# Running a step's three Q or K products in one go, with residual adds drawn apart and splits of x behind them, in a graph attention kernel

## The reference, cut to what matters

```python
def reference(x, adj, Wq, bq, Wk, bk, Wv, bv, Wf, bf):     # x (128,128,384), adj (128,128,128) bool
    q, k, v = heads(x @ Wq + bq), heads(x @ Wk + bk), heads(x @ Wv + bv)      # 6 heads of 64
    scores = einsum('bhqd,bhkd->bhqk', q, k) / sqrt(64)
    probs  = softmax(scores + where(adj, 0, -9e15)[:, None])
    ctx    = einsum('bhqk,bhkd->bhqd', probs, v)            # heads joined again to 384
    return layernorm(x + ctx @ Wf + bf)                     # over the 384, eps 1e-5, no affine
```

## Time and profile before

| | |
|---|---|
| median of 3 runs | 1035.22 us (1034.44 to 1036.75) |
| the profiled execution, its own time | 1036.09 us |
| its span, first to last instruction | 1034.2 us |
| TensorE busy | 98% of the span, 7161 matmuls |
| VectorE, ScalarE, GpSimd busy | 71%, 57%, 61% |
| mean granted TensorE clock | 0.997 of full |
| DMA | 179.6 MB, 174 GB/s in the mean |

### The profile page before, as it was taken

One profiled execution on the slowest core, in us unless ns is written; L12 is line 12 of the kernel. 1 busy time (PEld: TensorE's weight loads), 2 busy tenths in 40 slices (PEclk: granted clock), 3 DMA queues, 4 the chain that ended last, 5 costly groups with the idle time before them and its releaser, 6 DMA issues.

```text
span 1034.2 us, 26752 instructions
## 1 busy us (share of the span) xinstructions
PE 1018.6 (98%) x7161; PEld 906.7 (88%) x7161; DVE 734.0 (71%) x2826; ACT 592.9 (57%) x2119; POOL 626.8 (61%) x649
## 2 busy tenths in 40 slices
PE   8999999999999999999999999999999999999995
PEld 7889889888889888888898898898898898888885
DVE  3677776777677677777777777767776777776775
ACT  4565655655656646646556556556556466466551
POOL 1355666666656665665656656666566566656674
PEclk9999999999999999999999999999999999999998
DMA  7386676676676676666666766766766766765444
GB/s 196 79 210 178 173 197 163 176 189 163 177 190 163 180 189 166 186 181 167 189 174 172 194 167 173 196 162 175 191 161 174 195 164 182 185 167 171 152 141 139
DMA packets 340570, 179.63 MB, mean 174 GB/s; under 512 B 222656, under 2 KB 324160, under 8 KB 340544
## 3 DMA queue, kind: packets, MB, share of 16 engines
q1 hardware_dynamic: 339744, 178.94, 63.4%
q10 hardware_dynamic: 800, 0.39, 0.1%
HBM read 103.75 MB, written 75.50 MB: 173 GB/s over the span
## 4 chain that ended last, share of the span: by engine, by line
PE 96%; DVE 1%; DMA 1%; ACT 0%; issue 0%; POOL 0%; SPq 0%; POOLq 0%; DVEq 0%; ACTq 0%
PE qk_ps L377 14%; PE qk_ps L379 13%; PE qk_ps L378 13%; PE cov_ps L377 13%; PE cov_ps L379 13%; PE cov_ps L378 13%; PE scores_ps L393 9%; PE cov_ps L408 9%; DMA p_out<-p_turned 1%; DVE s_mask L572 1%; PE qk_ps L468 0%; POOL probs L870 0%; SPq L289 0%; DVE xT_lo L561 0%; ACT probs L755 0%
## 5 line engine op out<-in xcount | busy, mean ns | idle before, releaser
L755 ACT ACTIVATE probs<-s_mask,neg_max 128x128 f32<-128x128 f32 x768 | 297.5, 391 | 6.2 <-DVE neg_max L578 5.5
L870 POOL TENSOR_TENSOR probs<-probs,inv_sum 128x768 f32<-128x768 f32 x128 | 188.9, 1476 | 81.5 <-DVE inv_sum L591 81.5
L572 DVE CUSTOM_DVE_ANT_0 s_mask<-scores_ps,mask_bias 128x128 f32<-128x128 f32 x768 | 172.5, 286 | 91.5 <-PE scores_ps L393 86.5
L865 POOL TENSOR_SCALAR y_sb<-y_sb,mean_var,rstd 128x384 f32<-128x384 f32 x124 | 204.9, 1652 | 22.9 <-POOL rstd L859 22.9
L584 DVE STREAM_TRANSPOSE p_turned<-probs 128x768 f32<-128x768 f32 x128 | 125.2, 978 | 114.2 <-POOL probs L870 114.0
L859 POOL TENSOR_TENSOR rstd<-var_eps,minus_half 128x1 f32<-128x1 f32 x128 | 72.0, 563 | 181.8 <-DVE var_eps L619 181.8
L772 ACT ACTIVATE qT<-qk_ps,bq_col 128x512 f32<-128x512 f32 x96 | 65.5, 682 | 155.5 <-PE qk_ps L379 155.5
L755 ACT ACTIVATION_READ_ACCUMULATOR probs<-s_mask,neg_max 128x1 f32 x768 | 145.0, 189 | 0.0
L748 ACT CAST cT_hi<-cov_ps 128x384 fp32r<-128x384 f32 x128 | 61.5, 480 | 137.2 <-PE cov_ps L408 134.3
L561 DVE TENSOR_TENSOR xT_lo<-xT,xT_hi 128x384 fp32r<-128x384 f32 x120 | 113.1, 980 | 32.8 <-ACT xT_hi L742 32.7
L377 PE MATMUL cov_ps<-wf_hi,cT_hi 128*128 128x384 f32 x384 | 129.9, 338 | 1.7 <-DVE cT_lo L546 1.7
(11 more groups left out here) (64 smaller groups left out, 1988.5 us busy)
## 6 DMA issues: line engine op xcount, KB each, us to landing
p_out<-p_turned SPq DMA_DIRECT2D x128, 384.0 KB, 2.6
pT<-p_out SPq DMA_DIRECT2D x512, 96.0 KB, 2.4
x_in<-in_x SPq DMA_DIRECT2D x128, 192.0 KB, 3.6
out<-y_sb SPq DMA_DIRECT2D x128, 192.0 KB, 2.5
x_blocks<-in_x SPq DMA_DIRECT2D x360, 64.0 KB, 2.3
adj_u<-in_adj SPq DMA_DIRECT2D x32, 64.0 KB, 3.4
probs<-in_L_gnn_Wv SPq DMA_DIRECT2D x1, 576.0 KB, 6.2
pT<-in_L_gnn_Wf SPq DMA_DIRECT2D x1, 576.0 KB, 6.7
```

The lines of the kernel that those rows point to most:

```text
L572: last = nc.vector.tensor_tensor_reduce(out=s_mask[:, e, h, :], in0=scores_ps[:, score_cols(e, h)], in1=mask_bias[:, e, :], scale=SCALE, s ...
L755: last = nc.scalar.activation(probs[:, e, h, :], s_mask[:, e, h, :], ACT.Exp, bias=neg_max[:, e, h:h + 1], scale=1.0, accum_out=row_sum[:, ...
L865: nc.gpsimd.tensor_scalar(y_sb[:, y, :], y_sb[:, y, :], mean_var[:, e, 0:1], rstd[:, e, 0:1], ALU.subtract, ALU.mult).then_inc(y_ready, 1)
L870: nc.gpsimd.tensor_tensor(probs[:, e, :, :], probs[:, e, :, :], inv_sum[:, e, :].unsqueeze(2).broadcast_to([P, HEADS, SEQ]), ALU.mult).the ...
```

## The change

Three edits. TensorE issues all three Q or K jobs of a step right after the context products; the out products follow, and V right behind those. VectorE adds residual 0 right after the second inversion of sums, then turns the blocks of e = 1, then adds residual 1; the two splits of x come behind that, and both `find_stats` after them at the end of the step. Other engines' programs, all buffers and all waits are as they were; `ending` is as it was.

```diff
@@ TensorE, step
-                for j in jobs[:2]:
+                for j in jobs:
                     qk_product(i, c, j)
                 if isinstance(p, int) and by_matmul(2 * (p + X_AHEAD)):
                     for e in range(2):
...
                 if real(p - LAG, PAIRS):
                     for e in range(2):
                         out_product(c, p, e)
-                for j in jobs[2:]:
-                    qk_product(i, c, j)
                 if real(p + AHEAD, ENDING):
                     for e in range(2):
                         early_v(c, p, e)
@@ VectorE, step
                     invert_sums(0, 2 * p)
                     turn_blocks(i, c, 0, 2 * p)
                     invert_sums(1, 2 * p + 1)
+                if real(p - LAG, PAIRS):
+                    add_residual(i, c, 0, 2 * (p - LAG))
+                if real(p, PAIRS):
+                    turn_blocks(i, c, 1, 2 * p + 1)
+                if real(p - LAG, PAIRS):
+                    add_residual(i, c, 1, 2 * (p - LAG) + 1)
                 if real(p + X_AHEAD, PAIRS):
                     for e in range(2):
                         split_x(c, e, 2 * (p + X_AHEAD) + e)
...
                 if real(p - LAG, PAIRS):
                     for e in range(2):
-                        add_residual(i, c, e, 2 * (p - LAG) + e)
-                    find_stats(c, 0, 2 * (p - LAG))
-                if real(p, PAIRS):
-                    turn_blocks(i, c, 1, 2 * p + 1)
-                if real(p - LAG, PAIRS):
-                    find_stats(c, 1, 2 * (p - LAG) + 1)
+                        find_stats(c, e, 2 * (p - LAG) + e)
```

## The result

The changed kernel takes 1039.18 us (median of 7 runs, 1037.64 to 1040.97), against 1034.68 us for the kernel before (7 runs, 1034.22 to 1036.75): ratio 1.0038, 95% interval 1.0029 to 1.0047. It is slower by 0.4%. Predicted were 1037.6 us and slower: +2.4 us on the median then known (1035.22), where +4.5 were measured (1034.68 to 1039.18). The profiled execution took 1040.04 us, its span is 1038.2 us, 4.0 longer than before.

A forecast was written before the change was run, and what follows sets the result against it. TensorE, busy 98% of the span, was taken to bound the kernel. Terms -4.1 + 1.85 + 2.2 + 2.4 = +2.35 gave 1038.45 us profiled, 1037.6 us as median; range 1033.0 to 1041.8.

The forecast's parts named there:

- Middle steps, -4.1: Steps 2 to 60: two width changes fewer per step, 0.07 us each step for 59 steps; bounds 0 and 4.7.
- The rival without this gain: Middle steps: 2.04 and 2.09 differ by place, not by the neighbour's width; 1041.7 us, chance 0.14.
- The waits of the middle, 0: Middle steps: copy, residuals, splits, statistics and GpSimd's later variance all stay hidden; cost 0.
- The ring over GpSimd: Middle steps: rival with a VectorE-GpSimd ring of about 15.85 us if splits still take 1.88; 1046 us, chance 0.08.
- The front, +1.85: Step -2: third job ahead of the transposes delays their chain to the first V product; bounds 1.5 and 2.1 us.
- The rule: Middle splits: two-SBUF-input VectorE and SBUF-reading GpSimd instructions exclude each other; moved pair takes 1.1 us, otherwise up to 1.9.
- The clock in the front: Front's longer idle time: a clock fall would add up to 2 us, outside the forecast's sum.
- The ending, +2.2: Steps 60 to 62: late statistics and GpSimd variance put the first mask of 62 at 993.2 against 991.03.
- the lower bound 0.4: Ending: lower bound of the +2.2 term, with GpSimd's delay absorbed.
- The clock in the ending, +2.4: Out product of 62: clock expected to fall after 4.8 us idle in place of 1.74; bounds 0 and 3.2.
- The sum: Whole kernel: -4.1 + 1.85 + 2.2 + 2.4 = +2.35 us against the profiled execution's 1036.09, so 1038.45.

The follow-up runs named there:

- the kernel with five changes: Kernel before with middle steps laced (job, out 0, job, out 1, job, V), five width changes a step in place of three; 1039.62 us, ratio 1.0035.
- TensorE's order alone: Kernel before with TensorE's new order throughout and VectorE's old order; 1041.41 us, ratio 1.0063.
- TensorE's ending back: Changed kernel with only TensorE's steps 60 and 61 in the order of before; 1037.90 us, ratio 1.0023.
- GpSimd held back: Changed kernel, but GpSimd rounds Wf only after VectorE has split Wv; 1038.26 us, ratio 1.0021.
- The two engine-by-engine runs: Changed kernel with steps 60 and 61 in the order of before on one engine only: TensorE's 1037.90 us, VectorE's 1039.16 us.
- VectorE's order alone: Kernel before with VectorE's new order throughout and TensorE's order of before; 1038.57 us, ratio 1.0026.
- both ends back: Changed kernel with steps before 0 and steps 60 and 61 in the order of before; 1032.02 us, ratio 0.9971.
- the kernel with dummy transposes there: Changed kernel with both ends in the order of before, plus 24 dummy transposes ahead of the last pair's context products; 1030.96 us, ratio 0.9953.
- VectorE's ending back: Changed kernel with only VectorE's steps 60 and 61 in the order of before; 1039.16 us, ratio 1.0035.

## Why the prediction was right, step by step

- **Middle steps, -4.1.** Measured -3.86 in the profiled executions (58 steps, not 59, at 0.067 in the mean and not 0.07). The step of 15.61, the third job at 2.04, no wait of TensorE: all as said. The reason, a cost of each change of width, held in the kernel with five changes, with the reserve on roles made there. The rival without this gain is out. The Trainium skill, page TensorE: Matmul & The Clock Gate, section "Back-to-back issue gap", gives an isolated gap by the moving operand's length alone. That formula does not describe the stream here, where the neighbour counts by 26 to 41 ns over nine matmuls.
- **The waits of the middle, 0.** Right: 0.8 us spare at V, 0.76 at the mask, splits 0.55 each. The ring over GpSimd did not close, even with the splits at 1.87 (VectorE's order of before under TensorE's new one): 15.63. Its price had been made too high.
- **The front, +1.85.** This step failed in size in the profiled execution: +2.46. The working moved the splits of Wv later at their old 1.49 us, and did not ask what GpSimd does at the new time. There they met the rounding of Wf and took 2.11. In the two traces in which they ran ahead of it (TensorE's order alone, TensorE's ending back), and with GpSimd held back, they took 1.49 and TensorE's wait ahead of V grew from 0.89 to 2.70, by 1.81, as worked out; in the three in which the rounding began first it grew to 3.33, 3.46 and 3.63. So the chain was right and +1.85 is its lower case. The rule had been cited for the middle, where it helps, and not carried to the place where it can hurt.
- **The clock in the front**, named only as up to 2 us on top of the forecast, did fall: V took 4.82 in place of 3.26, +1.56, and 4.80 to 5.61 in four other traces with the new front. It belonged in the sum with the same reason as in the ending: the idle time was worked out as 2.75, longer than the 2.47 after which the trace of before shows a fall.
- **The ending, +2.2.** Measured +2.0 (18.18 to 20.18 from the scores of 61), by the chain given: statistics directly ahead of the mask, and GpSimd back to back from the late variance (978.24, before 976.15) to the first probabilities of step 61. The first mask of 62 came at 993.02, predicted 993.2; the two can be compared because front and middle happened to cancel (+0.04 at the scores of step 60). Two sums of the working are a little off without harm: 976.55 + 0.54 + 1.94 is 979.03 and not 979.15, and the lower bound 0.4 should read 0.55. The two engine-by-engine runs show that both halves of the change have a part.
- **The clock in the ending, +2.4.** Measured +1.55 for that product, within the bounds of 0 and 3.2: the clock came back after ten of its eighteen matmuls. In three of the six traces with a wait of 4.20 to 4.30 the product was slow almost throughout, at +2.6 to +2.7.
- **The sum.** +2.35 was predicted against the profiled execution, +3.95 measured (1036.09 to 1040.04). The two terms of the front make 2.2 more, the clock in the ending 0.85 less, the rest is small. By medians the slowdown is 4.5, nearly twice the forecast; the direction and the mechanism were right, and the range was wide enough for what the front's two terms lacked. That the ending's clock term was too large in this execution, and hid part of it, is luck.

## What to carry to other kernels

An order that is better in the loop need not be better in the written-out steps at its ends, where work that covered a chain is missing; keep the old order there, and both gains are had (ratio 0.9971 in place of 1.0038). When a VectorE instruction with two SBUF inputs is moved in time, look at what GpSimd does at the new time, not only at the old. An idle stretch of TensorE should be priced twice, once as the wait and once for a possible half-speed product behind it: every unfilled wait of 3.3 us or more in these traces was followed by a fall, nine of nine, and between 1.8 and 2.9 us some were and some not. Dummy matmuls in the wait took the second price away.

## What the runs showed of the hardware that was not expected

A product of nine matmuls is paced by what ran before it: 2.081 against 2.040 us for 512 columns, 1.586 against 1.56 for 384 columns. The middle steps of the changed kernel all take 15.613 or 15.614 us; those of the kernel before lie between 15.66 and 15.69. And the length of an idle stretch does not alone decide whether the clock falls. Ahead of V the same wait of 2.70 us was followed by a fall in two traces and by none in a third. Ahead of the out product of 62 it fell after 2.86 (TensorE's ending back, 4.89 for the product) and held after 2.57 (VectorE's order alone, 3.33). Near the end it fell after 2.47, after 2.88 with both ends back, and after 1.78 in the kernel with dummy transposes there. The cost of a fall varies as well, +1.4 to +2.7 for the same product after the same wait. So the same kernel spreads from run to run, by up to 5.2 us (VectorE's ending back: 1038.26 at a mean granted clock of 0.995, 1043.45 at 0.989). What decides between these was not tried.
